# The first 20 microseconds of an attention and feed-forward kernel: ones multiplied until the first input comes, the first context batch loaded and split in two halves, and VectorE's and ScalarE's start in another order

## The reference

```python
def xattn(q, k, v, Wq, Wk, Wv, Wo, bo, g):      # 8 heads of 64
    qh = (Wq q).reshape(b, 8, 64, n); kh = (Wk k)...; vh = (Wv v)...
    qh = softmax(qh, axis=-2) * 64 ** -0.5       # over the head's 64 rows
    kh = softmax(kh, axis=-1)                    # over the 1024 positions
    context = einsum('bhdn,bhen->bhde', kh, vh)
    out = einsum('bhde,bhdn->bhen', context, qh) # then Wo, bo
    return out / norm(out, axis=1) * g * sqrt(128)

x = x + xattn(layernorm(x), ctx, ctx, ...)
x = x + ffn(layernorm(x), ...)    # top-8 routing over 256 slots, a value mixture, a gate
```

## Time and profile before

| | before |
|---|---|
| median of 3 runs | 653.26 us |
| profiled execution, own time | 652.88 us |
| its span, first to last instruction | 651.1 us |
| TensorE, VectorE busy | 620.2, 578.3 us |
| ScalarE, GpSimd busy | 419.3, 372.5 us |
| mean granted TensorE clock | 0.997 |

### The profile page before, as it was taken

The page is one execution under the profiler, slowest core; times in us unless marked ns, Lnnn a source line. Parts: engine busy times, 40 slices in busy tenths (PEclk is TensorE's granted clock), DMA queues, the critical chain, the costliest instruction groups (busy, mean ns, idle before and its releaser), DMA issues.

```text
span 651.1 us, 11774 instructions
## 1 busy us (share of the span) xinstructions
PE 620.2 (95%) x3974; PEld 543.0 (83%) x3974; DVE 578.3 (89%) x788; ACT 419.3 (64%) x844; POOL 372.5 (57%) x291
## 2 busy tenths in 40 slices
PE   4899999999999999999999999999999899999796
PEld 3778888888888888888888888888879799998574
DVE  5999899999999999999999999999997646866996
ACT  5475766666666666766666666666665756583793
POOL 4954464746565656565656565564555656652394
PEclk9999999999999999999999999999999899999999
DMA  8843434343434343434344443433252100000056
GB/s 310 219 107 107 146 99 129 105 132 103 133 100 131 103 136 105 131 102 134 100 139 134 114 125 104 130 100 100 72 182 60 41 2 2 1 1 1 33 221 264
DMA packets 52011, 72.57 MB, mean 111 GB/s; under 512 B 10112, under 2 KB 42400, under 8 KB 51696
## 3 DMA queue, kind: packets, MB, share of 16 engines
q1 hardware_dynamic: 50912, 68.07, 35.3%
q0 software_dynamic: 896, 2.45, 1.2%
q10 hardware_dynamic: 144, 1.31, 0.6%
HBM read 29.85 MB, written 8.39 MB: 59 GB/s over the span
## 4 chain that ended last, share of the span: by engine, by line
PE 45%; DVE 30%; issue 19%; ACT 2%; DMA 2%; SPq 2%; DVEq 0%; POOL 0%; ACTq 0%; POOLq 0%
PE gm L475 10%; DVE qsum L1116 7%; DVE qm L1106 7%; PE ob L498 6%; PE gm L550 5%; PE turn L550 4%; DVE qs_sb L1109 3%; DVE nkm L1085 3%; DVE st L1071 3%; DVE st L1131 2%; PE q_slot L433 2%; PE turn L506 2%; DVE kt L1092 2%; PE k_slot L433 2%; PE k_slot L435 2%
## 5 line engine op out<-in xcount | busy, mean ns | idle before, releaser
L959 POOL TENSOR_TENSOR qs_sb<-qs_sb,qrec 128x1024 f32<-128x1024 f32 x64 | 122.0, 1907 | 202.5 <-DVE qrec L1120 202.5
L730 ACT ACTIVATE ek<-k_slot,nkm 128x1024 f32<-128x1024 f32 x62 | 69.0, 1114 | 100.9 <-DVE nkm L1085 100.8
L498 PE MATMUL ob<-mt_sb,q_hd 128*128 128x128 f32 x1024 | 126.4, 277 | 0.6 <-ACT o_sb L752 0.5
L498 PEld LDWEIGHTS ob<-mt_sb,q_hd 128*128 128x128 f32 x1024 | 121.8, 192 | 5.2 <-issue 3.6
L475 PE MATMUL gm<-ekT,ctxT 128*128 128x256 f32 x512 | 118.2, 379 | 1.6 <-issue 1.6
L475 PEld LDWEIGHTS gm<-ekT,ctxT 128*128 128x128 f32 x512 | 97.0, 190 | 16.5 <-issue 2.0
L740 ACT ACTIVATE qs_sb<-qs_sb 128x1024 f32<-128x1024 f32 x64 | 68.4, 1069 | 41.6 <-DVE qs_sb L1109 41.6
L1085 DVE TENSOR_REDUCE nkm<-k_slot 128x1 f32<-128x1024 f32 x62 | 74.2, 1197 | 13.3 <-PE k_slot L435 13.3
L1109 DVE TENSOR_TENSOR qs_sb<-q_slot,qm 128x1024 f32<-128x1024 f32 x64 | 78.4, 1225 | 2.2
L1116 DVE TENSOR_REDUCE qsum<-qs_sb 128x16 f32<-128x1024 f32 x64 | 76.9, 1201 | 3.0 <-ACT qs_sb L740 3.0
L1092 DVE STREAM_TRANSPOSE kt<-ek 128x1024 f32<-128x1024 f32 x64 | 78.5, 1227 | 0.0
(11 more groups left out here) (196 smaller groups left out, 1272.9 us busy)
## 6 DMA issues: line engine op xcount, KB each, us to landing
ekT<-kt SPq DMA_DIRECT2D x496, 64.0 KB, 2.0
ctx_in<-ctx_rows SPq DMA_DIRECT2D x16, 512.0 KB, 4.6
x_all<-x SPq DMA_DIRECT2D x16, 512.0 KB, 3.6
ctxT<-ctx_cols SPq DMA_DIRECT2D x16, 512.0 KB, 4.0
out<-q_hd SPq DMA_DIRECT2D x15, 512.0 KB, 2.6
Wuq_in<-Wuq_cols ACTq DMA_DIRECT2D x1, 1280.0 KB, 5.7
x_all<-values_cols POOLq DMA_DIRECT2D x1, 1024.0 KB, 7.2
ekT<-kt POOLq DMA_DIRECT2D x16, 64.0 KB, 4.4
```

The lines of the kernel that those rows point to most:

```text
L498: last = nc.tensor.matmul(ob[:, (j % 4) * C:(j % 4 + 1) * C], q_hd[:, t, j * P:(j + 1) * P], mt_sb[:, b % 2, t, :], start=(t == 0), stop=( ...
L959: nc.gpsimd.tensor_tensor(e, e, qrec[:, i % 2, :].unsqueeze(2).broadcast_to([P, PAIR, DH]), ALU.mult).then_inc(q_mul, 1)
```

## The change

At the start, TensorE multiplies `ones` by `ones` twelve times into `gm`, which nothing reads before its next use (`run_up`). The first context is loaded by two DMAs of 256 KB, split by two ScalarE copies and two VectorE subtractions, with semaphores of their own; the first half of tile 0 is multiplied when the first half is split. ScalarE takes the first k exponential and then `WqT_hi` ahead of the layernorm of x, and has one more k exponential ahead of `x_high`. VectorE takes the first k maximum ahead of x's statistics, the second ahead of x's bias, each later transpose ahead of the next maximum, and the low part of `WqT` after three transposes. Tile (1, 0) waits for three k exponentials instead of four. The orders on GpSimd and SyncE stay, but for the first context's second DMA; the load of ctx for batch 1 also waits for the two new semaphores.

```diff
             def load_ctx(b):
                 wait(sp, ctx_hi_done, b)
                 wait(sp, ctx_lo_done, b)
+                if b == 1:
+                    sp.wait_ge(ctx_first_hi, 1)
+                    sp.wait_ge(ctx_first_lo, 1)
                 sp.dma_start(ctx_in[:, :], ctx_rows[b]).then_inc(ctx_loaded, 16)
...
-            load_ctx(0)
+            sp.dma_start(ctx_in[:, 0:HALF], ctx_rows[0][:, 0:HALF]).then_inc(ctx_first_in, 16)
+            sp.dma_start(ctx_in[:, HALF:N], ctx_rows[0][:, HALF:N]).then_inc(ctx_loaded, 16)
...
+            def run_up():
+
+                pe.wait_ge(consts, 2)
+                for n in range(12):
+                    nc.tensor.matmul(gm[:, 0:P], ones[:, :], ones[:, :], start=True, stop=True)
+
             def k_tile(b, i):
-                pe.wait_ge(ctx_lo_done, b + 1)
-                wait(pe, k_exp, 4 * b + i - (b == 0))
+                if 4 * b + i == 0:
+                    pe.wait_ge(ctx_first_lo, 1)
+                else:
+                    pe.wait_ge(ctx_lo_done, b + 1)
+                wait(pe, k_exp, 4 * b + i - (4 * b + i <= 4))
                 for n in range(2):
                     cols = slice(n * HALF, (n + 1) * HALF)
+                    if 4 * b + i == 0 and n == 1:
+                        pe.wait_ge(ctx_lo_done, 1)
...
+            run_up()
             pe.wait_ge(k_weights, 2)
...
+            weights_high(WkT, WkT_in, k_weights_in, k_weights)
+            act.wait_ge(ctx_first_in, 16)
+            nc.scalar.copy(ctx_hi[:, 0, 0:HALF], ctx_in[:, 0:HALF]).then_inc(ctx_first_hi, 1)
+            act.wait_ge(ctx_loaded, 16)
+            nc.scalar.copy(ctx_hi[:, 0, HALF:N], ctx_in[:, HALF:N]).then_inc(ctx_hi_done, 1)
+            k_exponential(0, 0)
+            weights_high(WqT, WqT_in, q_weights_in, q_weights)
             x_layernorm(0)
-            k_exponential(0, 0)
+            k_exponential(0, 1)
             ctx_high(1)
-            k_exponential(0, 1)
+            k_exponential(0, 2)
             x_high(0)
-            k_exponential(0, 2)
             k_exponential(0, 3)
...
             weights_low(WkT, WkT_in, k_weights)
+            dve.wait_ge(ctx_first_hi, 1)
+            V.tensor_tensor(ctx_lo[:, 0, 0:HALF], ctx_in[:, 0:HALF], ctx_hi[:, 0, 0:HALF].bitcast(F32),
+                            ALU.subtract).then_inc(ctx_first_lo, 1)
             dve.wait_ge(ctx_hi_done, 1)
-            V.tensor_tensor(ctx_lo[:, 0, :], ctx_in[:, :], ctx_hi[:, 0, :].bitcast(F32),
+            V.tensor_tensor(ctx_lo[:, 0, HALF:N], ctx_in[:, HALF:N], ctx_hi[:, 0, HALF:N].bitcast(F32),
                             ALU.subtract).then_inc(ctx_lo_done, 1)
+            k_maximum(0, 0)
             x_statistics(0)
+            k_maximum(0, 1)
+            x_bias(0)
+            for i in range(2, 4):
+                k_turn(0, i - 2)
+                k_maximum(0, i)
+            k_turn(0, 2)
             weights_low(WqT, WqT_in, q_weights)
-            x_bias(0)
-            k_maximum(0, 0)
-            for i in range(1, 4):
-                k_maximum(0, i)
-                k_turn(0, i - 1)
```

More of the change, by code:

```diff
@@ L253, in attention_ffn_kernel @@
         x_split = sem("x_split")
+        ctx_first_in = sem("ctx_first_in")
+        ctx_first_hi = sem("ctx_first_hi")
+        ctx_first_lo = sem("ctx_first_lo")
         ctx_hi_done = sem("ctx_hi_done")
@@ L809, in hidden_step, with weights_high @@
                     unit_sum(b - 1, (b - 1) % 2)
-            for weights, raw, come, done in ((WkT, WkT_in, k_weights_in, k_weights),
-                                             (WqT, WqT_in, q_weights_in, q_weights)):
+            def weights_high(weights, raw, come, done):
                 act.wait_ge(come, 16)
                 nc.scalar.copy(weights[0][:, :], raw).then_inc(done, 1)
-                if weights is WkT:
-                    ctx_high(0)
+            weights_high(WkT, WkT_in, k_weights_in, k_weights)
[5 more added lines that the diff above has]
+            weights_high(WqT, WqT_in, q_weights_in, q_weights)
             x_layernorm(0)
-            k_exponential(0, 0)
+            k_exponential(0, 1)
             ctx_high(1)
-            k_exponential(0, 1)
+            k_exponential(0, 2)
             x_high(0)
-            k_exponential(0, 2)
             k_exponential(0, 3)
```

## The result

The changed kernel took 655.84 us (median of 6 runs, 655.19 to 656.73) against 653.38 us of the kernel before in the same comparison (6 runs, 652.28 to 654.59): ratio 1.0042, 95% interval 1.0024 to 1.0061, so 2.5 us slower. Timed once more in another sitting, twelve runs beside 29 of before, it gave 656.88 against 653.28, ratio 1.0059, 1.0039 to 1.0080. The profiled execution took 655.19 us with a span of 653.4, that of before 652.88 with a span of 651.1.

A forecast was written before the change was run, and what follows sets the result against it. Two strands, k and x, bound the first 20 us, TensorE mostly after. Transpose (1,0) +1.9 us less 0.76 slack gave +1.2: 654.1 on the profiled execution, 654.4 likeliest as median, range 652.3 to 655.8.

The forecast's parts named there:

- Part 3: VectorE's transpose (1,0) waits for GpSimd's eighth move behind the earlier ctx load: 28.6 instead of 26.68, +1.9 us on VectorE.
- TensorE's slack: At TensorE's third q pair, 0.76 us between the end of the second q subtraction and its use, absorbing that much delay.
- Half two ... at 5.0 (to 5.5): Second half of the first ctx load lands at 5.0, at most 5.5, so the first k maximum runs 7.35 to 8.57.
- The first half, put at 4.3: First half of the first ctx load lands at 4.3, bounds 3.5 to 5.0.
- Rival C: Run-up brings no fast clock or ends at 6.4; first maximum and GpSimd's moves later: 655.6 to 656.3 us, chance 0.12.
- The landing: 5.1 taken: GpSimd's eighth move, issued at 23.5 behind the ctx load, lands 5.1 us later at 28.6; lower bound 2.5 us, 26.0.
- WqT_lo at 0.64 "under the cover of xn_lo": VectorE's low part of WqT, behind three transposes, ends near 19.0, its 0.64 us hidden by GpSimd's xn_lo.
- no later wait is tied to absolute time: After 42.88 VectorE's order has no wait to 63 us, so whatever the first 43 us gain or lose stays to the end.
- Part 1: Run-up and ctx halves: fast clock at about 5.1, tile 0 ends near 7.3 instead of 10.3; worth nothing in the end.
- Rivals A and B: A: moves land quickly, 652.4 to 653.0 us, chance 0.25. B: VectorE's 1.3 us lead passes whole, 651.1 to 652.0, chance 0.08.
- the forecast +1.2 at the third q pair: TensorE's third q pair waits for the second q subtraction: +1.9 less 0.76 slack, about +1.2 us, carried to the end.

The follow-up runs named there:

- The early: Kernel before with only SyncE's ctx load of batch 2 issued earlier, after its fifth move instead of its eighth: 655.12 us, ratio 1.0024.
- the small load: Changed kernel with the ctx load of batch 2 cut to 64 of 1024 columns, the batch computed from stale columns: 654.60 us, ratio 1.0010.
- experiments 7 and 8: Changed kernel, x's statistics before the first maximum; 7: moves shared 12 SyncE, 4 GpSimd, 654.55 us; 8: batch 2 ctx load behind SyncE's second eight moves, 654.43 us.
- experiment 3: Kernel before with only the twelve products of ones added on TensorE: 653.83 us, ratio 0.9991.
- experiment 12: Changed kernel without the twelve products of ones: 656.32 us, ratio 1.0050.
- experiments 6 and 10: Changed kernel, statistics before first maximum; 6: batch 2 ctx load cut to 64 columns, 654.09 us; 10: that load late and WqT_lo behind x's bias, 655.19 us.
- experiment 15: Changed kernel timed again without edits beside before, with a line fitted to time against mean granted clock: 656.88 us, ratio 1.0059.

## Why the prediction failed, point by point

- **Direction and mechanism of Part 3: right.** The wait named, VectorE's transpose (1,0) for GpSimd's eighth move behind an earlier ctx load, is the one that the chain of the changed kernel shows, 2.38 us. The early and the small load show the cause on either side, and with TensorE's slack the loss arrived where it was forecast, at the third q pair (+2.62 for +3.23 at the transpose, slack 0.61 instead of 0.76).
- **"Half two ... at 5.0 (to 5.5)": the step that failed.** It was in use at 6.26, 4.6 us after its issue, outside the bound. So the maximum ran 8.66 to 9.89, not 7.35 to 8.57, the statistics began at 9.80, not 8.57, and GpSimd's moves at 20.68, not 19.75: 0.93 of the miss. It was no accident of one execution: of the ten profiled ones with halves, nine have the second half in use after 5.5 (5.72 to 6.96, once 5.38). The first half, put at 4.3 (3.5 to 5.0), was in use at 4.12 to 4.74 in nine of the ten and at 5.04 in this one.
- **Rival C's time, by another cause.** By its own words C "decides as soon as the maximum ends later than 8.6"; it ended at 9.89, and C's 655.6 to 656.3 holds the median of 655.84. But C's cause, a slow clock in tile 0, did not come: the late load of the second half did the same to the maximum.
- **The landing: 5.1 taken, 5.4 measured**, +0.3, and in part luck. With the load issued ahead of the eighth move, other executions show 3.8, 3.9, 4.4, 4.5, 4.5 and 6.0, so a term with a spread of 2 us was treated as a number. In the second execution of the changed kernel it was 3.8, and transpose (1,0) began at 28.13, ahead of the forecast 28.6 although the moves began later.
- **WqT_lo at 0.64 "under the cover of xn_lo": wrong, without consequence in the changed kernel.** It took 2.19 because of xn_lo. The cover that counted was the wait for the moves; away from xn_lo the time did not fall. Only where VectorE no longer waits for the moves does it count: in experiments 7 and 8 it took 2.17 and 1.57, and (1,0) stood at 27.61 and 27.16.
- **No term for one more VectorE instruction:** +0.69 us, 390 us later. I had said that no later wait is tied to absolute time; these pauses are tied to the instruction's place in its engine's program, and the sum had nothing for them.
- **Part 1: right for TensorE** (full speed from the first matmul of tile 0). That it is worth nothing in the end holds against before (experiment 3); within the changed kernel the run-up keeps the x strand about 0.7 us earlier than it would be without (experiment 12).
- **Rivals A and B** are out: the transpose began 3.2 us after 26.7. The ctx load on SyncE's queue set the larger part of the landing on GpSimd's: 3.8 to 6.0 us in seven executions with it ahead, 2.2 to 2.4 in four without, but 3.4 and 3.5 in two more without (experiments 6 and 10), which nothing here explains. With the larger part agrees the Trainium skill, "DMA: Bandwidth & Descriptors", section "Queues, rings and completion order", by which a transfer's semaphore waits for earlier writes of the same DMA engine in whichever queue. No run here tells that rule from a mere sharing of the DMA engines' rate.

The sum corrected, for the profiled execution: the forecast +1.2 at the third q pair, +0.93 for the later moves, +0.3 for the landing and +0.15 for the smaller slack are the +2.6 measured there; the pauses add 0.7, and the later part, in which the clock dipped in the execution of before and not in this one, takes back 1.0. That is the 2.3 us between the spans; the medians say +2.5 and +3.6, the estimates at equal clock of experiment 15 +2.6 and +2.8.

## What to carry to other kernels

When one strand is made earlier, list what its end triggers, above all large loads on a queue whose DMAs share the engines with transfers that another, later strand waits for; the place of one load was worth 1.5 us, the whole rearrangement nothing. Before taking an instruction ahead of a critical one, bound its start by the latest landing that its inputs can have, and not by the likely one: of a transfer in two halves, the first half was in use before the whole had been in nine of ten executions, but the second, which the maximum needs, was later than the whole in all ten. Judge a start by positions in the trace that recur each period, since single times spread more than what is looked for, and compare medians together with the mean granted clock of their runs.

## What the runs showed of the hardware

- ctx loaded whole (512 KB) landed 3.7 to 3.8 us after its issue in seven executions. In two halves of 256 KB, the first landed in 2.9 to 3.8 us, the second in 3.7 to 5.3 (ten executions).
- 64 KB moves on GpSimd's queue landed in 3.8 to 6.0 us with a 512 KB load issued ahead on SyncE's (seven executions), and in 2.2 to 2.4, twice 3.4 and 3.5, without it.
- VectorE's 512-column subtraction took 0.64 to 0.69 us alone and 1.57 to 2.19 beside a GpSimd tensor operation, as x's bias takes 1.87 beside q's scaling.
- One more VectorE instruction at 4 us brought two pauses, 0.69 us with their surroundings, into the path at 389 and 455 us. What the engine does in them no run here shows.
- Two dips of the granted clock, to 0.96 and 0.91 over some 40 us each, made one execution 3.7 us longer than another of the same kernel in the part behind 478 us.
